# Flamingo block on one core, last stage: a third buffer for the rounded h, two residual buffers in place of three

## The reference, cut to what matters

```
x1 = x + tanh(g_xattn) * attention(layernorm(x), ctx)
xq = fake_quant(layernorm(x1))
h  = silu(xq @ quant(w_gate).T) * (xq @ quant(w_up).T)      # 1408 wide
s  = sigmoid(clip) * max|h| / 127                           # one number for the whole of h
hq = clip(round(h / s), -128, 127)
out = x1 + tanh(g_ffn) * (hq * s) @ quant(w_down).T
```

## Time and profile before

| | |
|---|---|
| median of 3 runs | 1687.38 us |
| profiled execution, its time | 1690.03 us |
| profiled execution, its span | 1687.9 us |
| mean granted TensorE clock | 0.986 |
| PE, DVE, ACT, POOL busy share of the span | 94%, 77%, 48%, 33% |
| the last stage: first rounding on ACT | 1512.38 us from the span's start |
| first and last matmul group of the last stage start at | 1515.03 and 1673.74 us |

### The profile page before, as it was taken

One profiled execution on the slowest core, in us unless ns is written; L12 is line 12 of the kernel. 1 busy time (PEld: TensorE's weight loads), 2 busy tenths in 40 slices (PEclk: granted clock), 3 DMA queues, 4 the chain that ended last, 5 costly groups with the idle time before them and its releaser, 6 DMA issues.

```text
span 1687.9 us, 30603 instructions
## 1 busy us (share of the span) xinstructions
PE 1579.9 (94%) x11464; PEld 739.6 (44%) x11510; DVE 1306.0 (77%) x2102; ACT 814.0 (48%) x1092; POOL 558.8 (33%) x782
## 2 busy tenths in 40 slices
PE   4899999999999999999999999997799999989988
PEld 2344444444444444454444544443344444434433
DVE  5648788788887878878788777776788888878865
ACT  4453633535335353363533525334477666758341
POOL 5423514335143352332523325023000000007978
PEclk9999999999999999999999999999899999999999
DMA  9688869788696875968879677545287765227997
GB/s 246 147 214 188 179 169 193 170 203 170 172 204 157 201 177 171 197 157 200 175 183 193 166 192 167 156 101 212 63 255 239 241 217 169 51 87 280 417 426 282
DMA packets 333748, 328.62 MB, mean 195 GB/s; under 512 B 209072, under 2 KB 258224, under 8 KB 330672
## 3 DMA queue, kind: packets, MB, share of 16 engines
q1 hardware_dynamic: 331888, 326.59, 72.4%
q10 hardware_dynamic: 1728, 0.27, 0.1%
HBM read 180.49 MB, written 100.27 MB: 166 GB/s over the span
## 4 chain that ended last, share of the span: by engine, by line
PE 67%; DVE 13%; ACT 7%; DMA 6%; issue 4%; SPq 2%; POOL 1%; POOLq 0%; ACTq 0%; DVEq 0%
PE spair L1624 17%; PE bank L1407 10%; PE bank L1519 10%; PE bank L1409 9%; PE bank L1408 9%; PE spair L1496 5%; PE bank L1650 4%; DVE mx L1047 4%; ACT pr L778 2%; PE spair L1471 2%; DMA out_dram<-yh 1%; ACT wf L848 1%; DMA ffn_work<-out_dram 1%; DVE bst L997 1%; DVE wi L1135 1%
## 5 line engine op out<-in xcount | busy, mean ns | idle before, releaser
L1047 DVE TENSOR_REDUCE mx<-spair 128x4 f32<-128x1024 f32 x256 | 301.2, 1218 | 35.2 <-PE spair L1471 34.7
L778 ACT ACTIVATE pr<-spair 128x1024 f32<-128x1024 f32 x256 | 258.2, 1020 | 113.5 <-PE spair L1496 113.5
L1024 DVE SCALAR_TENSOR_TENSOR parts<-bank,bqk,parts 128x512 f16<-128x512 f32 x128 | 96.0, 750 | 164.6 <-ACT parts L767 163.2
L1624 PE MATMUL spair<-ffn_work,wgT 128*128 128x512 bf16 x688 | 180.2, 382 | 2.2 <-ACT ffn_work L925 1.4
L1624 PE MATMUL spair<-ffn_work,wuT 128*128 128x512 bf16 x690 | 180.1, 381 | 0.7
L891 ACT ACTIVATE ffn_work<-spair,gsc 128x512 f32<-128x512 f32 x176 | 118.2, 680 | 102.5 <-PE spair L1624 102.4
L1496 PE MATMUL spair<-stacks 128*128 128x256 f16 x1024 | 152.7, 276 | 14.2 <-ACT pr L778 10.5
L767 ACT ACTIVATE parts<-bank,bqk 128x512 f16<-128x512 f32 x128 | 87.8, 686 | 156.1 <-PE bank L1409 156.1
L641 POOL TENSOR_TENSOR cl<-cbuf,ch 128x512 f16<-128x512 f32 x64 | 77.1, 1206 | 230.4 <-ACT ch L755 230.4
L1519 PE MATMUL bank<-pr,v 128*32 128x256 f32 x2048 | 137.9, 387 | 15.1 <-ACT pr L778 8.6
L656 POOL TENSOR_TENSOR nw<-rt 128x4 f32<-128x4 f32 x96 | 19.4, 202 | 371.5 <-DVE rt L992 366.5
(11 more groups left out here) (190 smaller groups left out, 3312.6 us busy)
## 6 DMA issues: line engine op xcount, KB each, us to landing
stacks<-qk_spill SPq DMA_DIRECT2D x384, 128.0 KB, 4.0
qk_spill<-parts SPq DMA_DIRECT2D x64, 512.0 KB, 4.7
h_spill<-hb SPq DMA_DIRECT2D x10, 2816.0 KB, 9.2
x<-out_dram SPq DMA_DIRECT2D x27, 1024.0 KB, 11.5
xbuf<-in_x_dram SPq DMA_DIRECT2D x16, 1024.0 KB, 7.5
cbuf<-in_ctx_dram SPq DMA_DIRECT2D x16, 1024.0 KB, 6.5
xres<-in_x_dram SPq DMA_DIRECT2D x16, 1024.0 KB, 5.8
out_dram<-xres SPq DMA_DIRECT2D x16, 1024.0 KB, 4.5
```

Of the source, the lines that this page charges most:

```text
L778: act.activation(pr[:, u % 4, :, :, :].rearrange("p a b q -> p (a b q)"), spair[u % 2][:, :, :].rearrange("p a q -> p (a q)"), ACT.Exp, sc ...
L1024: dve.scalar_tensor_tensor(out=parts[:, c, 2 * w + 1, :], in0=pj[(g + 1) % 3][:, :], scalar=bqk[:, w, c:c + 1], in1=parts[:, c, 2 * w, :], ...
L1047: dve.tensor_reduce(mx[:, h:h + 2, b, :], spair[u % 2][:, :, :].rearrange("p a (q k) -> p a q k", q=KH), AX_X, ALU.max).then_inc(max_done, 1)
L1624: last = pe.matmul(spair[k % 2][:, s, :], w[:, t, kc * P:kc * P + P], xqT[:, par, kc, :], start=(kc == 0), stop=(kc == KC - 1))
```

## The change

h's integers get a third place, for groups with m % 3 = 2. No free block of 5632 bf16 columns exists, so it is in two parts: `hq_a`, chunks 0 to 7, lies in the first half of ffn_work (until now the third residual buffer), and `hq_b`, chunks 8 to 10, in the end of yh behind the two y buffers. A group in that place is quantized in four passes (two of 4096 columns, two of 1536) in place of two.

DVE now makes the integers two groups ahead: after group 0 comes `h_quant(1)`, and then for each m `h_quant(m + 2)` and the four y tiles of m. Before, it was `h_quant(m + 1)`. The residual has two buffers (`r2s`), y keeps its three. SP's order becomes `load_res3(0)`, `load_res3(1)`, `load_h(0)`, `load_h(1)`, and then for each m `store_y(m)`, `load_res3(m + 2)`, `load_h(m + 2)`. PE's loop has three groups written out and then two rounds of six, since the place now goes by m % 3.

```
--- before.py
+++ after.py
@@ -264,7 +264,9 @@
         m2_all = sem("m2_all")
         h_in = [sem(f"h_in{n}") for n in range(5)]
-        r_in = [sem(f"r_in{n}") for n in range(3)]
+        r_in = [sem(f"r_in{n}") for n in range(2)]
+        ht_part = sem("ht_part")
+        hq_part = sem("hq_part")
         hr_first = sem("hr_first")
         ht_first = sem("ht_first")
         hq_first = sem("hq_first")
@@ -322,7 +324,19 @@
         y_two = yh[:, 0:2 * NT * D].rearrange("p (a t d) -> p a t d", a=2, t=NT)
         work_two = ffn_work[:, :].rearrange("p (a t d) -> p a t d", a=2, t=NT)
         y3 = [y_two[:, 0, :, :], y_two[:, 1, :, :], work_two[:, 1, :, :]]
-        r3 = [x2[:, 0, :, :], x2[:, 1, :, :], work_two[:, 0, :, :]]
+        r2s = [x2[:, 0, :, :], x2[:, 1, :, :]]
+        HA = NT * D // (G // 2)
+        hq_a = ffn_work[:, 0:NT * D].bitcast(BF16)
+        hq_b = yh[:, 2 * NT * D:2 * NT * D + (IC - HA) * G // 2].bitcast(BF16)
+        def hq_cols(place, kc, t):
+            if place < 2:
+                return hq[place][:, kc * G + t * P:kc * G + t * P + P]
+            part, k = (hq_a, kc) if kc < HA else (hq_b, kc - HA)
+            return part[:, k * G + t * P:k * G + t * P + P]
@@ -583,11 +597,12 @@
             group_of = ORDER + list(range(NS))
             def load_res3(m):
-                sp.dma_start(r3[m % 3], og[group_of[m]]).then_inc(r_in[m % 3], 16)
+                sp.dma_start(r2s[m % 2], og[group_of[m]]).then_inc(r_in[m % 2], 16)
             def load_h(k):
                 wait(sp, ht_done, k + 2 if k > 0 else 1)
+                wait(sp, ht_part, (k + 2) // 3 if k > 0 else 0)
                 sp.dma_start(RING[k % len(RING)], h_dram[k]).then_inc(h_in[k % len(RING)], 16)
             def store_y(m):
@@ -601,20 +616,17 @@
             load_res3(0)
             load_res3(1)
-            wait(sp, f_dma, (NG - 1) * 64)
-            wait(sp, gu_mm, (NG - 1) * 2 * IC)
-            load_res3(2)
             load_h(0)
+            load_h(1)
             for m in range(NG):
                 if m == NG - 1:
                     store_y_tiles(m)
                 else:
                     store_y(m)
-                if m + 3 < NG:
-                    load_res3(m + 3)
-                if m + 1 < NS:
-                    load_h(m + 1)
+                if m + 2 < NG:
+                    load_res3(m + 2)
+                if m + 2 < NS:
+                    load_h(m + 2)
             for b in range(3):
                 stores = len(range(b, NG, 3)) + (NT - 1 if (NG - 1) % 3 == b else 0)
                 wait(sp, y_out[b], 16 * stores)
@@ -730,10 +742,10 @@
             def add_res(m):
-                wait(pool, r_in[m % 3], 16 * (m // 3) + 16)
+                wait(pool, r_in[m % 2], 16 * (m // 2) + 16)
                 for t in range(NT):
                     wait(pool, y_scaled, m * NT + t + 1)
-                    pool.tensor_tensor(y3[m % 3][:, t, :], y3[m % 3][:, t, :], r3[m % 3][:, t, :], ALU.add).then_inc(y_ready, 1)
+                    pool.tensor_tensor(y3[m % 3][:, t, :], y3[m % 3][:, t, :], r2s[m % 2][:, t, :], ALU.add).then_inc(y_ready, 1)
             for m in range(NG):
                 add_res(m)
@@ -1344,12 +1356,25 @@
             dve.tensor_scalar(csb[:, :], csb[:, :], small[:, SH:SH + 1], small[:, TGF:TGF + 1],
                               ALU.mult, ALU.mult).then_inc(sc_step, 1)
-            def h_quant(n, par):
-                wait(dve, hr_done, n + 1)
-                wait(dve, d_mm, (n - 1) * NT)
-                dve.tensor_scalar(hq[par], h_read(n), MAGIC, QMAX, ALU.subtract, ALU.min).then_inc(ht_done, 1)
-                wait(dve, ht_done, n + 1)
-                dve.tensor_scalar(hq[par], hq[par], -QMAX - 1.0, None, ALU.max).then_inc(hq_ready, 1)
+            def h_quant(m):
+                wait(dve, hr_done, m + 1)
+                wait(dve, d_mm, (m - 2) * NT)
+                if m % 3 < 2:
+                    dve.tensor_scalar(hq[m % 3], h_read(m), MAGIC, QMAX, ALU.subtract, ALU.min).then_inc(ht_done, 1)
+                    wait(dve, ht_done, m + 1)
+                    dve.tensor_scalar(hq[m % 3], hq[m % 3], -QMAX - 1.0, None, ALU.max).then_inc(hq_ready, 1)
+                    return
+                if m == 2:
+                    wait(dve, f_dma, (NG - 1) * 64)
+                    wait(dve, gu_mm, NG * 2 * IC)
+                    wait(dve, ht_done, 2)
+                dve.tensor_scalar(hq_a, h_read(m)[:, 0:HA * G], MAGIC, QMAX, ALU.subtract, ALU.min).then_inc(ht_part, 1)
+                dve.tensor_scalar(hq_b, h_read(m)[:, HA * G:IC * G], MAGIC, QMAX, ALU.subtract, ALU.min).then_inc(ht_done, 1)
+                wait(dve, ht_part, m // 3 + 1)
+                dve.tensor_scalar(hq_a, hq_a, -QMAX - 1.0, None, ALU.max).then_inc(hq_part, 1)
+                wait(dve, ht_done, m + 1)
+                dve.tensor_scalar(hq_b, hq_b, -QMAX - 1.0, None, ALU.max).then_inc(hq_ready, 1)
             def y_tile(m, t):
                 wait(dve, d_mm, m * NT + t + 1)
@@ -1367,9 +1392,10 @@
                 wait(dve, ht_done if last else ht_first, 1 if last else k + 1)
                 dve.tensor_scalar(part, part, -QMAX - 1.0, None,
                                   ALU.max).then_inc(hq_ready if last else hq_first, 1)
+            h_quant(1)
             for m in range(NG):
-                if m + 1 < NG:
-                    h_quant(m + 1, (m + 1) % 2)
+                if m + 2 < NG:
+                    h_quant(m + 2)
                 for t in range(NT):
                     y_tile(m, t)
@@ -1642,12 +1668,14 @@
             pe.wait_ge(down_in, 16)
-            def down(n, par):
-                wait(pe, hq_ready, n + 1)
+            def down(m, place, thirds):
+                wait(pe, hq_ready, m + 1)
+                if place == 2:
+                    wait(pe, hq_part, thirds + 1)
                 for t in range(NT):
-                    wait(pe, y_scaled, (n - 1) * NT + t + 1)
+                    wait(pe, y_scaled, (m - 1) * NT + t + 1)
                     for kc in range(IC):
-                        last = pe.matmul(pbs[t][:, :], hq[par][:, kc * G + t * P:kc * G + t * P + P], wdT[:, kc, :],
+                        last = pe.matmul(pbs[t][:, :], hq_cols(place, kc, t), wdT[:, kc, :],
                                          start=(kc == 0), stop=(kc == IC - 1))
                     last.then_inc(d_mm, 1)
@@ -1660,10 +1688,11 @@
                                          start=(kc == 0), stop=(kc == IC - 1))
                     if b == IC:
                         last.then_inc(d_mm, 1)
-            down(1, 1)
-            with pe.Fori(1, NG // 2) as i:
-                down(2 * i, 0)
-                down(2 * i + 1, 1)
+            for m in range(1, 4):
+                down(m, m % 3, m // 3)
+            with pe.Fori(0, (NG - 4) // 6) as i:
+                for k in range(4, 10):
+                    down(6 * i + k, k % 3, 2 * i + k // 3)
 # ---- launch: one core; inputs and outputs as the reference has them ----
```

## The result

The changed kernel takes 1696.32 us (1693.74 to 1697.99, 5 runs) against 1687.38 us: ratio 1.0048, 95% interval 1.0034 to 1.0062, some 8 us slower. The prediction was 1690.1 us, between 1685.5 and 1694.5, with "within 0.2%" as the likeliest outcome. It was wrong: the kernel is slower than any time in the range, and the loss is clear of the noise.

A forecast was written before the change was run, and what follows sets the result against it. Transfers bound the middle (11.88 us a group against PE's 9.50), PE the last three groups. PE's group 15 starting at 1676.4 against 1673.74 gave +2.7 on the 1687.4 median: 1690.1 us, range 1685.5 to 1694.5.

The forecast's parts named there:

- late start: Start of the last stage: y(0) stands behind the four passes of h_quant(2) on DVE, 5.0 us later, at 1532.7.
- gate of y(11): Middle of the stage: y(11) waits for store(8) to land, at 1645.5 in place of 1640.52.
- vanished wait of y(12): Before group 13: store(9) lands at 1650.5 in place of 1652.40, too early to gate PE; the 2.38 us wait goes.
- rival (b): Middle of the stage: the shallower queue slows blocks to 12.34 us; +6.4, 1693.8 us; chance 0.25.
- (c): PE's group 13: a stretch at half clock follows its 1.6 us wait; +4.3, 1691.7 us; chance 0.13.
- (d): Early blocks: load 1 out of the way, 11.88 us a block, y(11) at 1642.3; -0.5, 1686.9 us; chance 0.13.
- (e): Whole stage: the change doesn't do what it says, start not late, time within 1 us of 1687.4; chance 0.04.
- signs of being wrong: Whole stage: first store not late, blocks at another pace than 11.88 us, or the gate of y(11) not the last.
- The end: PE's groups 12 to 15: group 15 starts at 1676.4 against 1673.74, +2.7 us, and what follows is the same.
- unseen costs: Effects bounded outside the sum, among them residual loads a block later, with 7 to 9 us in hand, priced at 0.
- turns of POOL: In h_quant(14): a POOL tile gets in at each of three pass boundaries, 1.22 us each, making it 8.7 us.
- rival (a): h_quant(14) and PE's last groups: no POOL turns between passes, no clock drop; +1.0, 1688.4 us; chance 0.13.

The follow-up runs named there:

- early residuals: Changed kernel with the residuals of groups 13 to 15 loaded early into free places of h; ratio 1.0013 against the kernel before.
- only the later loads: Kernel before with h loads 8 and 9 one round later in SP's queue, load 1 where it was; ratio 0.9976.

## Why the prediction was wrong

**What held.** The late start (5.0 us forecast; y(0) 16.60 and 21.57 us after the reduction), the first store (1542.52, forecast 1542.8), the landing of load 9 and the gate of y(11) to 0.2 us, the vanished wait of y(12), PE's group 15 0.9 us earlier than forecast. The queue kept 11.88 us a block although it was shallower, so rival (b), which I gave the most weight of the slow cases, did not occur; nor did the clock of (c): group 13 took 9.67 us after a wait of 0.61. In the early blocks two took 12.3 us, less than in the kernel before (12.6 and 12.5), but y(11) did not come at 1642.3, so (d) is out, and the late start excludes (e). Of the signs of being wrong only the last came, and mildly: y(14) waited for the landing of store(11) until 1671.38, without holding PE up. None of them looked at POOL's last adds.

**The step that failed** is the sentence at the end of "The end": "What follows (last tiles, adds, stores) is the same", with its twin in the unseen costs, where residual loads a block later were priced at 0. I priced them in the middle of the stage, where a residual that comes a block late only takes slack from a deep queue. (The slack was given as 7 to 9 us; 18.8 less 9 is 9.8, and no other term is named.) In the tail there are no h loads and no backlog, the groups come every 9.50 us, and POOL, which the middle left a block behind, should catch up at 4.9 us a group. It can't at that pace: with two buffers, residual m + 2 is loaded only after the add of group m and takes 7.7 to 8.3 us to land. A round of load and add, for groups 11 to 13 and again 13 to 15, is 8.1 or 7.7 + 4.9 + 0.4 us, 13.3 for two groups where the adds alone are 9.9. That is still less than PE's 19.0 for two groups, so POOL does gain on PE, but too slowly: its add starts 10.8 us after the first y tile of group 11 is ready, and 9.1 us after that of group 15, where the early residuals leave 2.0. Two runs show it from either side: early residuals take 5.8 us off the changed kernel (by the ratios 0.35%), and two buffers alone put 6.4 on the kernel before (0.44%).

**A smaller one.** The turns of POOL were 1.07 us each and not 1.22, so that y(12) came at 1655.74 and not at 1656.6. The Trainium skill (SBUF — State Buffer, section Who interferes with whom) says that of a VectorE instruction in a 2-port mode and a GpSimd one the first to issue holds the shared ports for its whole length and the other is blocked. The trace agrees in kind: three of four passes beside POOL are 1.07 us longer, and none when POOL was idle at the start. At the boundary between two passes that no wait separates POOL got its turn too (0.95 became 2.02 us). So rival (a) is out as well, though its other half, no drop of the clock in group 13, held.

**Start and tail don't add up.** The start's 5 us reach PE's group 15 as 2.0, since the gate of y(12) goes. Taking the start away (one group ahead) makes group 15 earlier by 3.7 to 4.4 us but puts h_quant(15) beside POOL's late adds, and gives much of it back. Of 7.7 us, 1.9 are left when only the tail is mended; when only the start is, 4.5.

What stays open: in which cases PE's clock falls after a wait of 2.2 us, which makes the group 1.6 to 1.7 us longer each time; and whether h two groups ahead would pay with three residual buffers. I had no place for a third one beside the third place of h, so that wasn't tried.

## What to carry to other kernels

Price a lost buffer in the tail as well as in the middle: where the deep queue is gone, a load that waits for its buffer's last reader puts its full latency into the reader's chain, once per turn of the buffer, and the end is late if that reader enters the tail behind. Where a queue is the bound and its stores free the buffers, move loads that are early behind stores that are late: that took 0.24% off this kernel with no buffer and no byte, and 0.36% with one load also moved into an idle stretch ahead of the first store.

## What the runs showed of the hardware

- In the tail, with at most one older load still under way, a 1 MB load issued right behind a 1 MB store let POOL start 7.5 to 8.3 us after its issue (residuals 13 to 15 of the changed kernel, 14 and 15 of the kernel before with two buffers); with the load ahead of the store 6.5, 7.2 and 6.7 us. By the pace of the full queue (11.88 us for 4864 KB) I estimate 5.0 for the two.
- POOL's tile gets in between two DVE passes even where nothing separates them, at 1.07 us (0.95 became 2.02 in h_quant(14) of the changed kernel).
- PE's clock fell to half level (granted 0.50) in the group after a wait of 2.2 us in some cases (11.26 to 11.36 us for the group) and not in others (9.67), even within one kernel: before, in groups 10 and 13 and not in group 12. After a wait of 2.70 us it stayed up in group 10 with only the later loads, and after one of 3.06 us it fell in group 10 of the kernel before with two residual buffers.
